# One quad of four, not one of two, for GpSimd: redistributing the input products of a Mamba scan kernel

## What is computed

```python
x_ssm = xs @ W_x
dt, Bm, Cm = jnp.split(x_ssm, [D_INNER, D_INNER + D_STATE], axis=-1)
dt = jax.nn.softplus(dt @ W_dt)
A_disc = jnp.exp(A[None, None] * dt[..., None])
Bx = dt[..., None] * Bm[:, :, None, :] * xs[..., None]
def step(h, inp):
    Ad_t, Bx_t, C_t = inp
    h = Ad_t * h + Bx_t
    y = jnp.einsum('bdn,bn->bd', h, C_t)
    return (h, y)
```

## Time and profile before

| | |
|---|---|
| median of 3 runs | 2204.61 us (2198.73 to 2207.08) |
| the profiled execution | 2197.51 us |
| its span, first to last instruction | 2195.8 us |
| busy: GpSimd (POOL) | 1884.4 us, 86% |
| busy: VectorE (DVE) | 1846.1 us, 84% |
| busy: TensorE matmul (PE) | 1604.0 us, 73% |
| busy: ScalarE (ACT) | 1412.9 us, 64% |

### The profile page before, as it was taken

One profiled execution on the slowest core, in us unless ns is written; L12 is line 12 of the kernel. 1 busy time (PEld: TensorE's weight loads), 2 busy tenths in 40 slices (PEclk: granted clock), 3 DMA queues, 4 the chain that ended last, 5 costly groups with the idle time before them and its releaser, 6 DMA issues. The chain is left out here.

```text
span 2195.8 us, 22816 instructions
## 1 busy us (share of the span) xinstructions
PE 1604.0 (73%) x5492; PEld 632.6 (29%) x5492; DVE 1846.1 (84%) x2054; ACT 1412.9 (64%) x2547; POOL 1884.4 (86%) x786
## 2 busy tenths in 40 slices
PE   7776878696878778686878786968788784452690
PEld 3222323232322223232323232323223230111690
DVE  2478998999999989899999989999989899996312
ACT  2576777767686868686777777676868685541121
POOL 0286999999999999999999999999999999960456
PEclk9898979798898979798989797989889796665795
DMA  2673466665666675857575756656666758327752
GB/s 91 167 182 78 107 143 137 145 153 127 154 140 140 142 157 111 179 111 162 114 155 124 149 131 144 153 131 152 139 138 141 148 115 175 77 75 241 243 126 62
DMA packets 168980, 305.14 MB, mean 139 GB/s; under 512 B 27648, under 2 KB 87810, under 8 KB 168864
## 3 DMA queue, kind: packets, MB, share of 16 engines
q1 hardware_dynamic: 137696, 240.13, 44.3%
q0 software_dynamic: 30784, 62.85, 15.9%
q10 hardware_dynamic: 384, 1.05, 0.2%
HBM read 77.82 MB, written 39.52 MB: 53 GB/s over the span
## 5 line engine op out<-in xcount | busy, mean ns | idle before, releaser
L1021 DVE TENSOR_TENSOR_SCAN room<-pa,carry,room 128x512 f32<-128x512 f32 x1024 | 1243.5, 1265 | 87.9 <-ACT pa L870 55.3
L1220 POOL TENSOR_TENSOR room<-room 128x2048 f32<-128x2048 f32 x256 | 1228.9, 4814 | 54.0 <-ACT carry L863 54.0
L870 ACT ACTIVATE pa<-room,neg_a 128x512 f32<-128x512 f32 x1024 | 694.7, 687 | 370.5 <-DVE room L1021 333.6
L518 PE MATMUL py<-room,blk 128*32 128x512 f32 x2048 | 333.1, 724 | 239.4 <-POOL room L1220 132.9
L1007 DVE TENSOR_TENSOR room<-room,pb 128x2048 f32<-128x2048 f32 x176 | 398.5, 2264 | 33.3 <-DMA room<-du 33.3
L1213 POOL TENSOR_TENSOR room<-room,b_rep 128x2048 f32<-128x2048 f32 x80 | 369.0, 4612 | 36.2 <-DVE room L1021 34.8
L582 PE MATMUL pp<-xs,w_dtx 128*128 128x512 f32 x512 | 246.5, 621 | 18.9 <-DVE du L950 11.6
L546 PE MATMUL pp<-xsp,w_conv 128*128 128x512 f32 x512 | 245.3, 613 | 8.5 <-ACT xsp L736 8.4
L538 PE MATMUL pp<-xnt,w_in 128*128 128x512 f32 x256 | 177.5, 831 | 99.8 <-ACT xs L743 88.3
L518 PEld LDWEIGHTS py<-room,blk 128*32 128x32 f32 x2048 | 44.7, 117 | 439.3 <-POOL room L1220 241.8
L1186 POOL TENSOR_TENSOR du<-du,xs 128x512 f32<-128x512 f32 x64 | 93.3, 1682 | 73.6 <-DVE du L959 73.6
(11 more groups left out here) (185 smaller groups left out, 1896.5 us busy)
## 6 DMA issues: line engine op xcount, KB each, us to landing
room<-du SPq DMA_DIRECT2D x1016, 128.0 KB, 2.4
du<-du POOLq DMA_DIRECT2D x56, 512.0 KB, 6.7
room<-in_L_ffn_w_dram SPq DMA_DIRECT2D x39, 512.0 KB, 7.2
room<-bc_scratch SPq DMA_DIRECT2D x64, 256.0 KB, 5.1
du<-late POOLq DMA_DIRECT2D x28, 512.0 KB, 6.1
combine_scratch<-zeros SPq DMA_DIRECT2D x16, 520.0 KB, 9.8
xt<-in_L_attn_x_dram SPq DMA_DIRECT2D x16, 512.0 KB, 4.3
b_rep<-bc_scratch SPq DMA_DIRECT2D x64, 128.0 KB, 3.9
```

The source lines that it names most:

```text
L518: mm = pe.matmul(py[32 * j:32 * j + 32, :], blk[:], h[:, quad % 4, j, :], start=(g == 0), stop=(g == 3), tile_position=(0, 32 * j))
L870: act.activation(pa[:, decay_bank(t), :], rep[:, c % 2, t % 4, 0, :], ACT.Exp, scale=neg_a[:, a_column(t):a_column(t) + 1]).then_inc(s_exp, 1)
L1021: v.tensor_tensor_scan(h[:, quad % 4, t % 4, :], pa[:, decay_bank(t), :], bq[:, quad % 2, t % 4, :], carry[:, par, t:t + 1], ALU.mult, ALU ...
L1220: pool.tensor_tensor(h[:, quad % 4], h[:, quad % 4], c_rep[:, par, quad % 4, :].unsqueeze(1).broadcast_to((P, 4, T)), ALU.mult).then_inc(s ...
```

## The change

GpSimd makes the inputs of quads 1, 5, 9, 13 (before: 1, 3, 5, 7, 9), VectorE those of the other twelve (before: eleven). Each of VectorE's products gets a spread of B of its own by TensorE: twelve matmuls a tile instead of five, alternately into two PSUM banks; each waits until VectorE has made the product that last read its bank, two products earlier. `add_ln` moves from slots 46 and 47 to 44, `u` of groups 0 and 1 from 50 and 51 to 48, `rep` of group 0 from 53 to 50, and the second `pow` from 45 to 49. The five semaphores of the spreads become one. The tables `FIRST` and `SECOND` of the first two tiles get the same new entries of `sel`, and nothing else.

```diff
-    pe_bc=(18, 19), act_bc=21, store_bc=22, load_c=23, load_b=60, sel=(58, 62, 103, 111, 115),
+    pe_bc=(18, 19), act_bc=21, store_bc=22, load_c=23, load_b=60, sel=(58, 62, 67, 71, 75, 79, 87, 91, 95, 103, 107, 111),
-    ln=44, rest=((36, 37), (52, 53)), add_e=(30, 42), add_rest=(38, 54), add_ln=(46, 47), u=(50, 51, 60, 61),
-    rep=(53, 63, 79, 95))
+    ln=44, rest=((36, 37), (52, 53)), add_e=(30, 42), add_rest=(38, 54), add_ln=(44, 44), u=(48, 48, 60, 61),
+    rep=(50, 63, 79, 95))
...
-    load=-13, pe_out=(10, 11, 12, 13, 16, 17, 19, 20), dve_z=(15, 22), stats=(24, 42), pow=(27, 45), z2=30, x1=32,
+    load=-13, pe_out=(10, 11, 12, 13, 16, 17, 19, 20), dve_z=(15, 22), stats=(24, 42), pow=(27, 49), z2=30, x1=32,
...
-VECTOR_QUADS = (0, 2, 4, 6, 8, 10, 11, 12, 13, 14, 15)
-POOL_QUADS = (1, 3, 5, 7, 9)
+VECTOR_QUADS = (0, 2, 3, 4, 6, 7, 8, 10, 11, 12, 14, 15)
+POOL_QUADS = (1, 5, 9, 13)
...
-SPREADS = ((0, 0, 0, 14), (2, 1, 2, 15), (3, 1, 11, 10), (1, 0, 13, 12), (2, 0, 14, 13))
+SPREADS = ((0, 0, 0, 14), (2, 1, 2, 15), (3, 0, 3, 0), (0, 1, 4, 2), (2, 0, 6, 3), (3, 1, 7, 4), (0, 0, 8, 6),
+           (2, 1, 10, 7), (3, 0, 11, 8), (0, 1, 12, 10), (2, 0, 14, 11), (3, 1, 15, 12))
+NSP = len(SPREADS)
...
             if quad == first:
-                v.wait_ge(s_brep[n], i + 1)
+                v.wait_ge(s_brep, NSP * i + n + 1)
```

More of the change, by code:

```diff
@@ L62 @@
     pe_dt=((15, 16), (23, 24), (30, 31), (37, 38)), abs=(17, 25, 32, 65), exp=(18, 26, 33, 65), o1=(18, 27, 34, 66),
-    pe_bc=(19, 20), act_bc=21, store_bc=25, load_c=26, load_b=27, sel=(28, 29, 103, 111, 115),
+    pe_bc=(19, 20), act_bc=21, store_bc=25, load_c=26, load_b=27, sel=(28, 29, 67, 71, 75, 79, 87, 91, 95, 103, 107, 111),
     ln=((19, 0, 1), (27, 1, 2), (77, 2, DC)), s=(20, 28, 79, 82), o2=(21, 29, 80, 83), o3=(22, 30, 81, 84),
@@ L71 @@
     pe_dt=((29, 30), (35, 36), (39, 40), (42, 43)), abs=(31, 38, 41, 45), exp=(32, 39, 42, 45), o1=(33, 40, 43, 46),
-    pe_bc=(33, 34), act_bc=35, store_bc=36, load_c=37, load_b=60, sel=(58, 62, 103, 111, 115),
+    pe_bc=(33, 34), act_bc=35, store_bc=36, load_c=37, load_b=60, sel=(58, 62, 67, 71, 75, 79, 87, 91, 95, 103, 107, 111),
     ln=((36, 0, 1), (48, 1, DC)), s=(38, 50, 53, 56), o2=(39, 51, 54, 57), o3=(40, 52, 55, 58),
@@ L321, in scan_layers @@
         d_bcs, d_crep, d_brep, s_brep = (sem("bc_stored"), sem("c_loaded"), sem("b_loaded"),
-                                         [sem(f"b_spread_{n}") for n in range(len(SPREADS))])
+                                         sem("b_spread"))
         s_abs, s_sp, s_ln, s_s, s_o2 = (sem("softplus_abs"), sem("softplus_exp"), sem("softplus_ln"),
@@ L591, in prep @@
                             pe.matmul(pb[:, bank, :], sel_b[b:b + 32, g, :], bc[b:b + 32, :], start=True, stop=True,
-                                      tile_position=(b, 0)).then_inc(s_brep[n], 1)
+                                      tile_position=(b, 0)).then_inc(s_brep, 1)
                 def post(t, j, par, second):
@@ L757, in prep @@
                         atleast(act, d_bcs, 16 * i)
-                        for n in range(len(SPREADS)):
-                            atleast(act, s_brep[n], i - 1)
+                        atleast(act, s_brep, NSP * (i - 1))
                         act.copy(bc[32 * par:32 * par + 32, :], pp[32 * par:32 * par + 32, :]).then_inc(s_free, 1)
```

## The result

| | before | changed |
|---|---|---|
| median | 2202.86 us (4 runs, 2198.73 to 2207.08) | 2321.41 us (4 runs, 2320.84 to 2323.08) |
| the profiled execution | 2197.51 us | 2323.08 us |
| its span | 2195.8 us | 2321.3 us |

The changed kernel is slower by 5.4%: the ratio is 1.0539, with a 95% interval from 1.0517 to 1.0562. The forecast was 2258 us, with a range up to 2284: the sign is right, and the size less than half of what came.

A forecast was written before the change was run, and what follows sets the result against it. A loop through four engines was taken as the bound: GpSimd's backlog in part A, copies of `rep` in part B. 92.9 + 27.3 = 120.2 us a tile, +3.6; with the ends +54, so 2258 us, range 2215 to 2284.

The forecast's parts named there:

- part A: Tile from VectorE's first product to the end of scan 47: 90.52 us, forecast to become 92.9.
- part B: Tile from the end of scan 47 to the next tile's first product: 26.03 us, forecast 27.3.
- the misread start of `u`: Part B: `u` taken to begin at its recorded 1135.92, 7.87 us after scan 47; forecast 9.1 after the change.
- the chain through `u`: Part B: scan 47, GpSimd's work up to `u`, SyncE's copies of `rep`, next first product; 9.1 + 18.2 us.
- Two more products for VectorE: Part A: VectorE also makes quads 3 and 7, 2 x 2.18 = 4.36 us more, with nothing hiding them.
- TensorE's seven more spreads: TensorE: 7 x 0.8 = 5.6 us a tile more on an engine busy 90.8 of 116.3; cost taken as nothing.
- The rival on spreads: Head of the tile: spreads hold TensorE and so ScalarE, another +3 us a tile, 2300 us; chance 0.05.
- GpSimd must be free at the end of scan 47: End of part A: GpSimd free at about 1127.8, just before scan 47 ends at 1128.05.
- VectorE's waits for quads 5 and 9 go: Part A: GpSimd's backlog gone, and with it VectorE's waits for these products, 2.0 us a tile.
- From `u` to the copies: Part B: from `u` to the next first product stays 18.16 us; bounds 14.6 and 18.9.
- The order of SyncE: SyncE: load of `xo` moves behind the copies, `b_rep` lands up to some 2 us later; cost nothing.
- The rival of VectorE filling up: Whole tile: the wait for `rep` vanishes, 114.4 us a tile, faster at 2179 us; chance 0.09.

The follow-up runs named there:

- experiment 4: Changed kernel with ten of the twelve spreads left out, TensorE keeping its waits for VectorE's products of all twelve: 2278.0 us.
- experiment 12: Changed kernel with SyncE's load of `xo` put back ahead of the copies of group 0: 2312.20 us, ratio 1.0502 to before.
- experiment 3: Changed kernel with ten of the twelve spreads left out and their waits too, quads 3, 7, 11, 15 using another group's B: 2279.1 us.
- experiment 10: Kernel before with eleven spreads of B a tile in place of five, quads and order unchanged: 2243.79 us, ratio 1.0187.
- experiment 6: Changed kernel with the head of the next layer norm six slots earlier (HEAD_AT 24 instead of 30): 2338.58 us.
- experiment 9: Changed kernel with quad 13's product given back to VectorE, with a thirteenth spread: 2260.49 us, ratio 1.0258 to before.
- experiment 5: Changed kernel with `u` of groups 0 and 1 ahead of the `states` of quad 11 on GpSimd: 2262.79 us.
- Experiment 7: Changed kernel with the second `add_rest` in slot 58 instead of 54: 2294.43 us.

## Why the prediction was right in sign and half the size

The forecast missed 5.0 us a tile (125.2 - 120.2): 3.6 in part A and 1.4 in part B. In part A, 3.4 are the spreads (96.5 - 93.1, experiment 4) and 0.2 the place of the load of `xo` (experiment 12). In part B, SyncE starts 1.1 us later than forecast (12.4 - 11.3): GpSimd was 2.1 late, and the misread start of `u` had put 0.95 too much into the forecast. The other 0.3 lie between SyncE's start and the first product, where the place of the load costs 0.5 (16.3 in place of 15.8, experiment 12). Two of the prediction's own signs of being wrong came: GpSimd was late at scan 47, and the waits for ScalarE grew by 3.8 us a tile (2.9 to 6.7). That the sign came out right is not luck, since the chain through `u` was as described, and without the ten spreads the period is still 122.1 us, against 116.5 before. But the misread start stood against the larger errors, and without it the forecast would have been further off.

- *Two more products for VectorE* stood: the work is 89.91 and 21.55 us, and without the spreads part A is 93.0 as forecast.
- *TensorE's seven more spreads.* This step failed: "I take nothing". It had two faults. A spread is two matmuls (384 in all for 16 tiles x 12), so the added work is 15.6 - 7.2 = 8.4 us a tile, not 5.6. And TensorE's share of busy time was taken as cover, where the question was which instruction stands behind a spread. TensorE works in its written order, ScalarE waits for it in slots 8 and 19, and VectorE for ScalarE. Experiments 3, 4 and 10 show it: 3.4 us for ten spreads, 2.8 for six. At 0.47 each, the seven added ones come to an estimated 3.3. The rival on spreads had the right engine, but the wrong place and reason: neither the head of the tile (2.5 us before, 3.1 now, 2.9 without the spreads) nor a wait for a bank.
- *GpSimd must be free at the end of scan 47.* This failed as well. The prediction worked back one instruction, from the carry of quad 10. The carry ends at 690.50, but the `states` end at 697.30 and so began at about 692.8, since from slot 32 on the product of quad 9, the `states` of quads 7 to 9, a `pow` and three DMA issues leave GpSimd no gap. Its 4.5 us less a tile helped only where it was idle anyway. In place of the forecast's 4.6 the product of quad 13 ends at 6.7; experiment 6 takes 1.8 us of that away.
- *VectorE's waits for quads 5 and 9 go.* They did. In their place came the one for quad 13, 2.1 us a tile, since it has to wait for scan 47 and is late by the same backlog: "it hardly waits there" was wrong. In the sum it costs little of its own, as VectorE waits for the copies afterwards (4.8 us a tile; 5.8 was forecast).
- *Part B: the chain through `u`.* The mechanism stood. The product ahead of `u` is worth 4.5 us of SyncE's start and 4.5 of part B (experiment 9), and `u` ahead of the `states` 4.7 (experiment 5).
- *From `u` to the copies* stood. SyncE's start to the first product is 16.3 us, 16.0 before: the meeting is as bad in the new order. Experiment 7 shows that it is the meeting.
- *The order of SyncE.* "Cost nothing" is wrong by 9 us here (2321.41 - 2312.20), and by 15 in the kernel with the new order alone (2189.41 - 2174.39).
- *The rival of VectorE filling up* was right about VectorE's work and wrong about what it waits for. The Trainium skill (Perfetto Trace Analysis, "Identifying the Most-Contended Engine") says to find the engine with the highest occupancy and optimize it first; this change relieves GpSimd, which was that engine, and the kernel got 5.4% slower. The rule says where to look first; what a relief is worth depended here on the waits of the others.

Tile 0, forecast at +2 us, took 139.3 in place of 132.7, and tiles 1 and 14 6.1 and 7.9 more: the ends lose somewhat less than the 8.7 us of a middle tile.

## What to carry to other kernels

Cover is a matter of place: before an instruction is costed at nothing, look at what stands behind it on its engine and who waits for that, slot by slot, for the matmuls of an engine that is not the fullest too. Before work is put ahead of a chain that leads to a DMA, find the last idle gap of that engine and count everything from there, since its idle time in earlier slots is no help. Last, test the parts of a combined change apart: here the new order, without the move of one load, was worth 1.2%, and the new division of quads cost 6.2%.

## What was not expected of the hardware

- One fp32 spread of 32 x 512 through a selector is two matmul records, 1.12 us together in the rows shown; ten of them a tile, on an engine busy for 81% of the time, cost 3.4 us of 125.
- An accumulating DMA of 512 KB that GpSimd issues beside 16 copies of 128 KB makes their reader start 4.2 us later (16.3 us after the first issue in place of 12.0). Their issue takes 12.1 us in place of 10.0, and the slowest lands in 5.9 us in place of 2.4.
- A load of 512 KB just behind the copies, which needs only 0.43 us to issue, makes the next 4 x 128 KB land in a median of 5.3 us in place of 3.8, and their reader, with 3.0 us of idle time a tile, waits 1.2 us a tile for it.
- A row of GpSimd behind a DMA issue begins up to 2 us before its work can: such products are recorded with 6.4 us in place of 4.5. The ends follow each other at 4.5 us (704.52 and 708.99).
